# Maxima one place earlier in a decoder's attention, and the row step of pair 6 behind the next tile's first scores

## The reference

```python
alignment = jnp.einsum('bhqd,bhkd->bhqk', inner, outer) / scale
attn_align = jax.nn.softmax(alignment, axis=-1)
attn = attn_align * aperture.transpose(0, 2, 1)[..., :, None] * expression.transpose(0, 2, 1)[..., None, :]
attn = attn / (attn.sum(axis=-1, keepdims=True) + 1e-08)
converged = jnp.einsum('bhqk,bhkd->bhqd', attn, v)
...
scores = jnp.where(mask[:, None] == 0, jnp.float32(-1000000000.0), scores)
attn = jax.nn.softmax(scores, axis=-1)
ctx = jnp.einsum('bhqk,bhkd->bhqd', attn, vh)
```

## Time and profile before

| | |
|---|---|
| median of three runs | 4229.67 us (4223.36 to 4236.55) |
| profiled execution | 4230.22 us, span 4228.4 us |
| TensorE busy | 3986.3 us (94% of the span) |
| VectorE, ScalarE, GpSimd busy | 58%, 40%, 40% |
| mean granted TensorE clock | 0.978 |
| attention scores (L911) | first start 116.8 us, last 3226.3 us |
| row steps on mm, masked layer | first start 1641.7 us |

### The profile page before, as it was taken

One profiled execution on the slowest core, in us unless ns is written; L12 is line 12 of the kernel. 1 busy time (PEld: TensorE's weight loads), 2 busy tenths in 40 slices (PEclk: granted clock), 3 DMA queues, 4 the chain that ended last, 5 costly groups with the idle time before them and its releaser, 6 DMA issues. The chain is left out here.

```text
span 4228.4 us, 56968 instructions
## 1 busy us (share of the span) xinstructions
PE 3986.3 (94%) x20456; PEld 2322.0 (55%) x20456; DVE 2446.3 (58%) x4051; ACT 1685.3 (40%) x3099; POOL 1704.9 (40%) x1187
## 2 busy tenths in 40 slices
PE   7999999999999998999899989998998699999998
PEld 5444643654374455445544454455443488888886
DVE  4562555356346645675567466745673566666664
ACT  2454355345425533443344334433443322222322
POOL 0222221321222143765476537753763244444343
PEclk9999999999999999999999999999999799999998
DMA  3331322242133234223422342234210400000000
GB/s 102 76 74 50 105 58 56 71 105 62 60 92 77 69 131 112 54 69 125 115 54 68 125 115 54 67 126 115 54 36 27 146 31 31 31 27 30 27 31 13
DMA packets 175705, 303.61 MB, mean 72 GB/s; under 512 B 55296, under 2 KB 73344, under 8 KB 175424
## 3 DMA queue, kind: packets, MB, share of 16 engines
q1 hardware_dynamic: 164928, 282.66, 24.9%
q10 hardware_dynamic: 10496, 17.31, 1.1%
HBM read 154.13 MB, written 43.77 MB: 47 GB/s over the span
## 5 line engine op out<-in xcount | busy, mean ns | idle before, releaser
L1073 ACT ACTIVATE probs_a<-half_a 128x512 f32<-128x512 f32 x2048 | 1123.9, 595 | 998.5 <-PE half_a L914 459.8
L911 PE MATMUL half_a<-stack_a 97*128 97x512 f32 x2048 | 860.7, 478 | 38.1 <-ACT probs_a L1073 25.9
L1290 DVE TENSOR_REDUCE mx_a<-wide_a 128x1 f32<-128x1024 f32 x512 | 605.8, 1221 | 433.7 <-PE wide_a L867 430.4
L1286 DVE CUSTOM_DVE_ANT_0 wide_a<-wide_a,mask_q_a 128x1024 f32<-128x1024 f32 x512 | 620.3, 1245 | 314.7 <-PE wide_a L867 310.2
L867 PE MATMUL wide_a<-stack_a 96*128 96x512 f32 x2048 | 666.7, 431 | 31.4 <-DVE mx_a L1286 11.9
L911 PEld LDWEIGHTS half_a<-stack_a 97*128 97x128 f32 x2048 | 376.0, 193 | 569.1 <-ACT probs_a L1073 334.1
L766 POOL TENSOR_TENSOR psums_a<-psums_a,probs_a 128x1024 f32<-128x1024 f32 x232 | 560.8, 2438 | 128.1 <-ACT probs_a L1073 113.4
L1645 PE MATMUL work_e<-w_in_e,x_e 128*128 128x512 f32 x2304 | 570.1, 399 | 11.4 <-DVEq L1871 11.4
L850 PE MATMUL acc_a<-probs_a,v_a 128*32 128x512 f32 x4096 | 552.4, 610 | 2.5 <-ACT u_a L1058 2.3
L867 PEld LDWEIGHTS wide_a<-stack_a 96*128 96x128 f32 x2048 | 378.1, 193 | 207.8 <-issue 85.1
L1645 PEld LDWEIGHTS work_e<-w_in_e,x_e 128*128 128x128 f32 x2304 | 427.3, 190 | 111.4 <-DVEq L1871 12.4
(11 more groups left out here) (241 smaller groups left out, 4297.9 us busy)
## 6 DMA issues: line engine op xcount, KB each, us to landing
stack_a<-qk_a SPq DMA_DIRECT2D x336, 256.0 KB, 4.5
y_a<-x SPq DMA_DIRECT2D x8, 2048.0 KB, 8.6
x<-y_a SPq DMA_DIRECT2D x8, 2048.0 KB, 10.0
mstage_a<-mask SPq DMA_DIRECT2D x32, 512.0 KB, 4.2
mstage_a<-mask_t SPq DMA_DIRECT2D x32, 512.0 KB, 3.8
den_a<-denominators SPq DMA_DIRECT2D x252, 64.0 KB, 2.1
stack_a<-first_a SPq DMA_DIRECT2D x48, 256.0 KB, 5.1
stage_a<-x_t SPq DMA_DIRECT2D x20, 512.0 KB, 3.6
```

What stands on the lines that cost most here:

```text
L911: last = pe.matmul(bank[:, :], stack[0:3 * DH + 1, s, 2 + h, kt * P:(kt + 1) * P], stack[0:3 * DH + 1, s, h, c * CH:(c + 1) * CH], start=T ...
L1073: act.activation(probs[:, kt % 2 * 2 + h, c * CH:(c + 1) * CH], bank[:, :], ACT.Exp, scale=SCALE).then_inc(free, 1)
L1286: dve.tensor_tensor_reduce(bank[:, :], bank[:, :], mask_q[:, t, :], 1.0, -3e38, ALU.add, ALU.max, mx[:, p % 3, n:n + 1]).then_inc(free, 1)
L1290: dve.tensor_reduce(mx[:, p % 3, n:n + 1], bank[:, :], AX.X, ALU.max).then_inc(free, 1)
```

## The change

Tile 1 of pair 0 takes three units of maxima instead of two, and tile 6 of pair 5 none instead of one. All units between stand one place earlier in the list of steps. The row step of pair 6 no longer has a rule of its own: it is put behind the next tile's first scores, as for the other pairs.

```diff
-MAXIMA = ((0, 2, 3, 3, 3, 3, 3, 2),) + ((2,) * 8,) * 3 + ((2, 2, 2, 2, 2, 2, 3, 3),) + ((2, 3, 3, 3, 3, 3, 1, 0), (2, 2, 2, 2, 1, 0, 0, 0), (0,) * 8)
+MAXIMA = ((0, 3, 3, 3, 3, 3, 3, 2),) + ((2,) * 8,) * 3 + ((2, 2, 2, 2, 2, 2, 3, 3),) + ((2, 3, 3, 3, 3, 3, 0, 0), (2, 2, 2, 2, 1, 0, 0, 0), (0,) * 8)
...
             steps += [("pv", *before, part) for part in parts] + late
-            if p == 5:
-                steps += due
-                due = []
             if masked and kt not in DIRECT[p]:
```

## The result

The changed kernel takes 4265.22 us in the median of six runs (4258.17 to 4270.44), the kernel before 4227.55 us in six (4223.36 to 4236.55): ratio 1.0084, 95% interval 1.0073 to 1.0095. It is slower by about 37 us, as forecast (4266, range 4246 to 4278). The profiled execution took 4269.70 us (span 4267.9), 39.5 more than that of before.

The account below looks back on a forecast made before the run. TensorE, busy 94% of the span, was taken as the bound. Terms 3.4 + 8.3 + 14.0 - 1.5 + 7.2 + 2.0 + 2.8 = +36.2 us on 4229.7 gave 4265.9 us, range 4246 to 4278.

Parts of the forecast that it names:

- 1. The third maxima: Tile 1 of pair 0: third unit costs 0.85 us a plain batch, +3.4 in four; nothing in masked batches.
- 2. The wait for stack 6: Tile 0 of pair 5: pair 6's first unit waits for its stack's third copy, +8.3 us plain, +14.0 masked.
- 3. The row steps in tile 6: Masked pairs 1 to 3, tiles 6 and 7: mm and normalising step wait for GpSimd's additions, 0.6 each, +7.2 us.
- The plain row waits inside the pairs: Plain pairs: with row steps in tile 6, four waits for the late row go, -1.5 us.
- 4. The row of pair 6: Tiles 6 and 7 of pair 5: row step still waits, for the late unit or mm; plain zero, masked +2.0 us.
- The clock: TensorE's clock falls after three of pair 5's new waits at 1.4 us, the old fall gone: +2.8 us.
- rival D: The clock falls after all eight waits in pair 5: +7.0 us over the sum, 4273 us; chance 0.13.
- A: Not slower: masked VectorE order improves, mm runs in 0.17 us, waits vanish; +6.8, 4236 us; chance 0.07.
- B: Pair 6's copies land before the second unit, within 2.4 us of the third issue; +19.7, 4249 us; chance 0.04.
- C: Masked normalising step gets in between two GpSimd additions, so the row steps cost nothing; +24.6, 4254 us; chance 0.26.
- E: Whole kernel faster by over 0.3%, needing A and no wait for stack 6; chance 0.02.

Follow-up runs that it names:

- e9: Changed kernel with six extra matmuls, results unused, in tile 0 of pair 5 during TensorE's wait for the copies; 4258.59 us, 1.0065 of before.
- e5: Changed kernel with the small operation mm made by a reduction over pairs instead of an operation against a constant; 4255.56 us, 1.0052 of before.
- e7: Changed kernel with the masked layer's two normalising steps one tile later, in tiles 6 and 7; 4266.26 us, 1.0079 of before.
- e11: Kernel before, reordered so only pair 6's units begin one place earlier, its row step behind the next tile's first scores; 4260.10 us, 1.0081 of before.
- e1: Changed kernel with the old rule for pair 6's row step, put out at the end of tile 5 of pair 5; 4286.51 us, 1.0135 of before.
- e3: Changed kernel with pair 6's first unit back in tile 1 of pair 5 and one unit again in tile 6; 4223.43 us, 0.9985 of before.
- e10: Changed kernel with the edits of e3 and e5 together; 4201.15 us, 0.9934 of before.
- e4: Kernel before with three units in tile 1 of pair 0 and one instead of two in its tile 7; 4227.63 us, 1.0000 of before.

## Why the prediction was right

The sum of 36.2 came out as 39.5 in the profiled execution and 37.7 in the medians. The mechanisms were the ones named, but for the normalising step in pairs 1 and 3. Several sizes were off, the clock's most of all, and they cancelled: that the total fits to 2 us is luck, while the direction and the place of the loss are not.

**1. The third maxima.** Plain: +2.9 where 3.4 was forecast; kernels with the same pair 0 lie between -0.7 and +3.2, those with the old one between -1.5 and 0, so about 2 is likelier. Tile 1 itself bears that out. Where the clock was down in it once and equally long, it takes 5.70 to 5.75 us with two units and 6.28 to 6.34 with three, in all kernels here: 0.6 a batch and not 0.85. It is 0.6 in the masked layer too (5.25 before and 5.86 after, at nearly full clock), where the prediction had nothing. For the whole of masked pair 0 zero was forecast and -5.1 measured, but kernels with pair 0 as before also went down, by up to 5.4, so whether the third unit gains anything there stays open.

**2. The wait for stack 6.** Plain: 2.15 us in the batch whose clock did not fall, forecast 2.08; this holds to a tenth. Masked: the sum is right and the split is not. Forecast were 2.9 for the landing and 0.6 for copies issued later. Measured were some 1.6 us in tile 0 (7.49 in e9 against 5.85) and some 1.8 in pair 4. The forecast had VectorE's delay fall into the wait. It did overlap, but the other way round: TensorE waits for the bank behind the scores that release the copies, and so the copies get ahead by 1.4 us. Without the clock that makes about 6.0 in tile 0 and 7.5 in pair 4, 13.5 against 14.0. e5, e7 and e11 show the same from the other side: each takes the lag away or never makes it, and the wait for the copies grows from 16.0 to 19.5, 22.2 and 22.1 us.

**3. The row steps in tile 6.** The masked pairs 1 to 3 cost +6.3 (5.5 in e1 and e3, which share this part), forecast 7.2; 1.1 of the 6.3 is a fall of the clock in the third batch's pair 2. In pair 2 the chain was as described: mm 2.04 us, normalising step 2.82 behind it. Tiles 6 and 7 take 10.31 to 10.33 in three batches against 9.46, +0.85 for a forecast 0.8. In pairs 1 and 3 the forecast failed: the normalising step got in between the additions, and the tiles cost 0.3. The forecast 0.6, chosen between two bounds for all twelve, is near the mean of two different cases. The Trainium skill (SBUF — State Buffer, SBUF: two separate sides) has the pair of ports that VectorE and GpSimd share as a lock held for a whole instruction, and in Who interferes with whom it says of `tensor_reduce` that it never contends on trn2. The trace agrees, but for pair 0's four: beside the additions the same numbers by a reduction take 185 to 188 ns instead of 1735 in the median, and e10 is 22 us under e3. The plain row waits inside the pairs went as forecast. L908 from 500 to 1600 us, where before it had 0.8 in two, has one left, and that stands at the start of a batch (884.41):

```profile
  DMA stack_a<-mrow_a: 0.3, 1
```

But pairs 1 to 4 together give only -0.3, since single tiles in them scatter by as much as these waits.

**4. The row of pair 6.** Plain +0.2 (forecast 0), masked +2.0 (forecast +2.0). The masked match is luck: the steps make +0.8, and the rest is the clock, which the forecast had in another term and at this place as a gain of 1.4. TensorE still waits 2.17 us there, forecast 2.1; TensorE and VectorE, second masked batch, tile 6:

```profile
2322.00 0.38 PE L872 MATMUL wide_a<-neg_eye_a,mm_a 128*16 128x128 f32 x2 [2.17 <-DVE mm_a L1138]
```

```profile
2320.33 1.53 DVE L1138 TENSOR_SCALAR mm_a<-mx_a 128x16 f32<-128x16 f32 x1
```

**The clock** is the term that was mis-sized: three falls at 1.4 us had been taken, and seven of the eight batches fell, six in tile 0 of pair 5 and one in pair 4, at 1.4 to 2.6 us each. Tile 0 alone has 14.4 - 8.6 = 5.8 in the plain and 10.5 - 6.0 = 4.5 in the masked batches. With 1.4 in pair 4 that is 11.7 us. The fall in pair 2 adds 1.1. Behind pair 6's row step the old fall did not go away: there were two, 1.2 us more than before. So the clock took 14.0 us instead of 2.8, more than rival D had for it. Masked pair 0 (-5.1), the rest of the program (-1.8), part 3 (5.2 without its fall for 7.2) and part 4 (0.8 for 2.0) hid most of the 11.2 that were missing. How often the clock falls behind pair 6's row step is not settled by this: the kernel before had one such fall, e4 with the same steps there had three.

**The rivals.** A needed mm under 0.5 us in most of the 16 rows of pairs 2 to 5; it was in one of them. With a fast mm (e5) the kernel is still 0.5% slower, for the stack wait does not depend on it. B is out: a copy took 4.6 us in the median. The Trainium skill's fit (DMA: Bandwidth & Descriptors, Anatomy of one DMA), which is for a transfer that GpSimd issues, gives 2.6 as an estimate for one such copy. The trace does not bear it out for SyncE's copies: six of them are issued one behind another here, and the DMA engines move 202 GB/s in that window. C is half right: the normalising step took 0.67 us behind mm in seven of eight places of pairs 1 and 3, and 2.82 in pairs 2 and 4, which alone keep most of part 3's cost. D came near: the clock fell behind six of the eight waits. E needed A.

What part 3 is worth by itself depends on part 2. e11 has the stack wait without the slow mm and is 31 us slower than before, the changed kernel has both and is 38 slower, though part 3 and pair 4's lag add 15 us in its table.

## What to carry to other kernels

A step moved one place earlier in a queue is priced by what it needs, not by what it does: here a unit of two matmuls, 0.7 us, in each of eight batches makes its tile 25 us longer in all because its operand lands two or three us after its new place, and the kernel that keeps it out of that place (e3) is 42 faster. Ask of each moved step when its last input arrives, and then ask whether the idle time is long enough to bring down the clock, which took 10 of the 25. Where it does, and the wait can't be avoided, work on the waiting engine that is thrown away can pay (e9).

Two waits in a row on one engine do not add up. Whoever shortens the first should look at whether the second is fixed to an outside event; e7 took 10 us of lag out of pair 4 and gained nothing, and the same edit of mm was worth 10 to 13 us beside the copies' wait and 22 without it.

A total that fits its forecast does not show that the terms do. Here it took stretches at a known clock to see that four terms were off.

## What the runs showed of the hardware

TensorE's granted clock fell after a single wait of 2.5 to 2.6 us in three of four plain batches, and in three of four masked ones after two waits of 1.3 and 1.5 us with 2.2 us of work between them. Six matmuls of some 0.28 us each at the start of the wait kept it at 1.00 in all eight.

In the changed kernel's trace a few hundredths of a microsecond decide what it costs when VectorE and GpSimd meet: a normalising step that started 0.01 us before GpSimd's addition took 0.68 and the addition 2.91; one that started 0.10 us after it took 2.82 and the addition 2.37.

A tensor-by-constant operation on 16 numbers a partition took 174 ns alone and up to 2182 beside GpSimd's additions; a reduction over 32 numbers, stored for the purpose, took 186 in the same place.
